# Query, key and value projections as five fp16 products of high and low parts instead of two fp32 ones

## The chip, the cores and the metric

The kernel runs on one core of one Trainium2 chip. The metric is the device time of one execution in microseconds (us); the time before is the median of three runs. The profile is one further execution.

## The reference, cut to what matters

Sixteen images of 192 channels on a 32 x 32 grid (1024 tokens) pass through three layers, each added to its input: a gated recurrent mix over rows and columns, a windowed attention, and a mixture of four experts of which two are chosen for each token. The change touches the first step of the attention:

```python
def _L1_attn_ref(x, Wq, bq, Wk, bk, Wv, bv, Wo, bo):   # x: LayerNorm over the 192 channels of each token
    H, D = (6, 32)
    WIN = 33
    def proj(W, b):
        return (x @ W + b).reshape(B, L, H, D).transpose(0, 2, 1, 3)
    Q, K, V = (proj(Wq, bq), proj(Wk, bk), proj(Wv, bv))
    ...
    # token 0 attends to all tokens; every other token to the 33 around it and to token 0
```

So per image three products of a 1024 x 192 matrix with a 192 x 192 matrix.

## The kernel before

**Images as a pipeline.** No scheduler orders the work: every engine has its own program, written out by hand, and semaphores join them. For image i the program runs `attention(i)`, then `experts(i)`, which works through four blocks of 512 routed tokens (24 chunks, each a first product `ffn1` into 768/6 = 128 hidden channels and a second, `ffn2`, out of them). Beside the chunks of image i, the generator `between(i)` prepares the next images: the rest of image i's attention, the group norm and the state projection (`project_states`, PROJ) of image i+2, and for image i+1 the token norm, its transposes, the windows, and the projections to queries, keys and values. `Slots` say at which step of `between` each part stands; the table `STEPS` says how many steps are taken after each half chunk. The last steps are taken at three per chunk. Images 0, 1 and 2 are prepared with no or few chunks beside them (`between(-1)`, `between(0)`, `between(1)`, where image 1 has one block only); the other 13 images are prepared beside 24 chunks.

**The projections before.** ScalarE writes the normed tokens to XN (128 tokens x 8 tiles x 192, fp32; line 787). TensorE waits for them (`xn1_ready`) and for the gates of image i+2 to have left its PSUM banks (`gu_ready`), and turns XN in two steps of eight transposes (`turn_mixed`, line 1493), halves j = 0, 1 of 96 channels. ScalarE copies half 0 and VectorE half 1 out of PSUM as overlapping windows (`windows`, lines 488 to 494): XW holds, for each of 11 blocks of 93 tokens, the 125 tokens around it and token 0, 126 columns. Then come 18 pieces (`project`, lines 1503 to 1519): 6 for Q and 6 for K, each 4 (or 3) blocks wide, 372 (279) or 504 (378) columns, with two products (j = 0, 1) of a 96-column weight each, and 6 for V, each two blocks of 126 tokens as the weight and the 192 columns of WV moving. Four PSUM banks take turns, so piece n waits for piece n-4 to be read. ScalarE reads the even pieces and VectorE the odd ones (`evacuate_piece`, lines 513 to 532), adding the bias.

**What stands around them.** In the last seven chunks the program of TensorE is: `ffn1` of chunk n, two pieces, `ffn2` of chunk n-1, one piece. `ffn2` waits for `split` on VectorE (HHI, HLO, lines 1054 and 1057), which waits for the gelu on ScalarE (line 810), which waits for `ffn1`. VectorE's order is split, then its pieces; ScalarE's is gelu, then its pieces. The chunks' own products are fp16 already, with high and low parts: five of 512 columns in `ffn1` (line 1532), twelve of 192 columns in `ffn2` (lines 1550 to 1552).

Of the kernel before, what the change touches and what calls it, by code (L numbers as in the profile page):

```python
# [67 lines left out]
def window_view(t, offset, dims):  # L68

    base = t[:]  # L70
    return bass.AP(tensor=base.tensor, offset=base.offset + offset, ap=[[base.ap[0][0], dims[0]]] + dims[1:])


def hybrid_kernel(nc, x, proj_w, y_wa, y_wb, y_scale, eye, gavg, cavg, norm_w, norm_b, g1_wT, g1_b, g2_wT, bias_row,
                  scan_v, scan_u, scan_a, wq, wk, wv, wo, bq, bk, bv, mask, w1, w2, b1, gate_w, gate_b, before, after,
                  consts, tri, out, powers, slots, weights):
    ctx = ExitStack()
    with ctx:
# [8 lines left out]
        EYEB = sb("EYEB", [128, QS], BF16)  # L87
# [8 lines left out]
        WQ, WK, WV, WO = (sb(n, [128, 2, C]) for n in ("WQ", "WK", "WV", "WO"))  # L96
# [106 lines left out]
        PSUM = ctx.enter_context(nc.psum_tensor("PSUM", [128, 8, 512], F32))  # L203


        with ExitStack() as setup:
# [276 lines left out]
        def windows(copy, j, part, give):  # L483

            if part == 0:
                copy(XW[0:HC, j, 1:NB - 1, 0:KW],
                     window_view(PSUM, j * T + QB - PAD + 1, [HC, [QB, NB - 2], [1, KW]]))
                return  # L490
            copy(XW[0:HC, j, 0, PAD - 1:KW], window_view(PSUM, j * T, [HC, [1, KW - PAD + 1]]))
            last = (NB - 1) * QB - PAD + 1
            copy(XW[0:HC, j, NB - 1, 0:T - last], window_view(PSUM, j * T + last, [HC, [1, T - last]]))
            copy(XW[0:HC, j, :, KW], window_view(PSUM, j * T, [HC, [0, NB]])).then_inc(give, 1)

# [1360 lines left out]
```

## Time and profile before

| | |
|---|---|
| median of 3 runs | 3102.83 us (3099.03 to 3105.12) |
| the profiled execution | 3101.95 us, its span 3100.2 us |
| TensorE (PE) busy | 2628.2 us, 85% of the span |
| VectorE (DVE) busy | 1836.3 us, 59% |
| ScalarE (ACT) busy | 1124.6 us, 36% |
| chain that ended last | PE 67%, DVE 19%, ACT 4%, issue 4% |

PE is a matmul, PEld a load of its stationary operand, which overlaps matmuls. Ends of matmuls are modelled and include their latency, so what a matmul costs in a row of them is the distance of the starts, not its duration. An fp32 matmul stands in the trace as two records. Lines are those of the kernel before.

### The profile page before, as it was taken

The page shows a single profiled execution, that of the slowest core. Times are in us where ns is not written, and L with a number is a line of the kernel's source. Part 1 is how long each engine was busy: PE and PEld are TensorE (multiplying, and loading weights), DVE is VectorE, ACT ScalarE, POOL GpSimd, SP SyncE. Part 2 cuts the span into 40 slices and gives each one's busy share as a digit, 9 for nine tenths or more (in the row PEclk, how much of TensorE's full clock was granted, in tenths as well). Part 3 has the DMA queues.
Part 4 walks back from the last instruction along what each step waited for, and adds up shares of the span by engine and source line. Part 5 has one row for each costly group of instructions (what it writes and reads, how often), then busy time and mean ns, then how long its engine had stood idle before and what let it go on. Part 6 is the DMA issues. An engine that isn't in the chain of part 4 may idle for free.

```text
span 3100.2 us, 49397 instructions
## 1 busy us (share of the span) xinstructions
PE 2628.2 (85%) x17619; PEld 1919.8 (62%) x17619; DVE 1836.3 (59%) x5182; ACT 1124.6 (36%) x3347; POOL 815.0 (26%) x656
## 2 busy tenths in 40 slices
PE   1359797999898999999898999999998989998397
PEld 0237575767676676667676666767576766766264
DVE  4345464656666565656666665756666666656354
ACT  0024243434343434434343434334343434343122
POOL 0000021223232322223232312232232322232344
PEclk9769788999999999998999999999989999999699
DMA  2430011324224242324333242423242241414464
GB/s 39 92 116 14 23 53 26 93 65 103 67 60 110 35 115 49 91 66 103 71 83 85 40 128 30 118 54 94 65 103 65 50 122 23 126 36 136 117 152 101
DMA packets 272628, 241.72 MB, mean 78 GB/s; under 512 B 209020, under 2 KB 250494, under 8 KB 261760
## 3 DMA queue, kind: packets, MB, share of 16 engines
q1 hardware_dynamic: 211648, 147.17, 17.8%
q0 software_dynamic: 50880, 52.59, 10.3%
q10 hardware_dynamic: 9856, 38.80, 3.9%
q8 instruction: 141, 2.31, 0.3%
q14 instruction: 103, 0.84, 0.1%
HBM read 133.29 MB, written 73.59 MB: 67 GB/s over the span
## 4 chain that ended last, share of the span: by engine, by line
PE 67%; DVE 19%; ACT 4%; issue 4%; DMA 1%; POOL 1%; SPq 1%; ACTq 0%; DVEq 0%; POOLq 0%
PE PSUM L1532 10%; PE PSUM L1509 9%; PE PSUM L1580 7%; PE PSUM L1602 5%; PE PSUM L1550 4%; PE PSUM L1518 3%; PE PSUM L1552 3%; PE PSUM L1551 3%; DVE HLO L1057 3%; PE PSUM L1448 3%; PE PSUM L1404 2%; PE PSUM L1592 2%; DVE HHI L1054 2%; PE PSUM L1445 2%; PE PSUM L1677 2%
## 5 line engine op out<-in xcount | busy, mean ns | idle before, releaser
L1532 PE MATMUL PSUM<-XT,WB 128*128 128x512 f16 x2010 | 522.8, 393 | 46.9 <-DMA META<-slots 43.5
L702 POOL DMA_INDIRECT out_dram<-Y,META x228 | 363.5, 1594 | 643.9 <-DVE Y L1081 517.6
L842 ACT ACTIVATE PSPT<-PSUM,NMX 94x126 f32<-94x126 f32 x1056 | 367.1, 358 | 370.8 <-PE PSUM L1592 188.0
L810 ACT ACTIVATE HF<-PSUM,WB 128x512 f32<-128x512 f32 x402 | 273.9, 685 | 526.6 <-PE PSUM L1532 525.7
L1550 PE MATMUL PSUM<-WB,HHI 128*128 128x192 f16 x1608 | 400.8, 249 | 48.7 <-DVE HLO L1057 47.5
L1551 PE MATMUL PSUM<-WB,HHI 128*128 128x192 f16 x1608 | 399.1, 248 | 0.0
L1552 PE MATMUL PSUM<-WB,HLO 128*128 128x192 f16 x1608 | 399.0, 248 | 0.0
L1054 DVE TENSOR_SCALAR HHI<-HF 128x512 f16<-128x512 f32 x402 | 172.3, 429 | 354.2 <-ACT HF L810 351.8
L1532 PEld LDWEIGHTS PSUM<-XT,WB 128*128 128x128 f16 x2010 | 197.3, 101 | 227.2 <-issue 47.1
L1580 PE MATMUL PSUM<-KBD,QT 128*94 128x378 f32 x704 | 308.4, 522 | 9.7 <-ACT PSPT L842 8.1
L1057 DVE SCALAR_TENSOR_TENSOR HLO<-HF,HHI 128x512 f16<-128x512 f32 x402 | 278.3, 692 | 13.8
L687 POOL DMA_INDIRECT slots<-XROW,IDX x256 | 251.7, 983 | 82.8 <-issue 76.3
L1602 PE MATMUL PSUM<-VW,PSPT 126*94 126x32 f32 x2112 | 220.5, 257 | 33.4 <-DVE PSPT L1092 32.3
L1602 PEld LDWEIGHTS PSUM<-VW,PSPT 126*94 126x94 f32 x2112 | 206.1, 175 | 53.4 <-DVE PSPT L1092 53.3
L1550 PEld LDWEIGHTS PSUM<-WB,HHI 128*128 128x128 f16 x1608 | 160.4, 100 | 125.4 <-issue 67.1
L1108 DVE TENSOR_REDUCE NMX<-PSUM 94x3 f32<-94x378 f32 x352 | 185.1, 543 | 72.9 <-PE PSUM L1583 70.5
L842 ACT ACTIVATION_READ_ACCUMULATOR PSPT<-PSUM,NMX 94x1 f32 x1056 | 209.3, 198 | 0.0
L1099 DVE TENSOR_TENSOR XW<-PSUM,RDEN 94x192 f32<-94x192 f32 x176 | 62.3, 354 | 197.6 <-PE PSUM L1602 195.1
L658 POOL TENSOR_TENSOR TR<-TV,MHALF 128x4 f32<-128x4 f32 x32 | 34.0, 1063 | 541.7 <-DVE TV L940 541.7
L1551 PEld LDWEIGHTS PSUM<-WB,HHI 128*128 128x128 f16 x1608 | 159.0, 99 | 20.6 <-issue 11.1
L1592 PEld LDWEIGHTS PSUM<-EYE,PSPT 94*126 94x126 f32 x1056 | 113.0, 150 | 83.0 <-issue 77.5
L1552 PEld LDWEIGHTS PSUM<-WB,HLO 128*128 128x128 f16 x1608 | 158.8, 99 | 0.3
(270 smaller groups left out, 4542.6 us busy)
## 6 DMA issues: line engine op xcount, KB each, us to landing
WB<-weights SPq DMA_DIRECT2D x67, 1600.0 KB, 6.9
XR<-in_x ACTq DMA_DIRECT2D x16, 768.0 KB, 5.2
out_dram<-X ACTq DMA_DIRECT2D x32, 384.0 KB, 3.0
weights<-WB ACTq DMA_DIRECT2D x4, 1600.0 KB, 6.1
GUP<-TGU SPq DMA_DIRECT2D x256, 8.0 KB, 1.8
slots<-XROW,IDX POOLq DMA_INDIRECT x256
out_dram<-Y,META POOLq DMA_INDIRECT x228, 3.6
HF<-in_w ACTq DMA_DIRECT2D x6, 384.0 KB, 4.6
```

The source lines that it names most:

```text
L687: pool.indirect_dma_start(slots[:, :].bitcast(I32), bass.IndirectOffsetOnAxis(IDX[:, k, t:t + 1], 0), XROW[:, t, :].bitcast(I32), None, bo ...
L702: pool.indirect_dma_start(out[:, :], bass.IndirectOffsetOnAxis(row, 0), Y[:, wslot(i, j), q, :], None, bounds_check=B * T + BS - 1, oob_is ...
L810: act.activation(HF[:, k % 2, :], PSUM[:, 4 + k % 2, :], ACT.Gelu, scale=1 / (X_UP * W_UP), bias=bias).then_inc(f["gelu_done"], 1)
L842: e = act.activation(PS[0:QS, n % 2, h, :], PSUM[0:QS, n % 2, h * KS:(h + 1) * KS], ACT.Exp, bias=NMX[:, b, n % 2, h:h + 1], accum_out=DEN ...
L1057: dve.scalar_tensor_tensor(HLO[:, k % 2, :], HF[:, k % 2, :], H_UP, HHI[:, k % 2, :], ALU.mult, ALU.subtract).then_inc(f["hl_ready"], 1)
L1509: mm = pe.matmul(PSUM[0:HC, n % 4, 0:width], W[:, j, oh * HC:(oh + 1) * HC], XW[:, j, b0:b1, keys], start=(j == 0), stop=(j == 1))
L1532: mm = pe.matmul(dst, WB[:, ws, w:w + 128], XT[:, xs, chunk, :], start=(n == 0), stop=(n == 4))
L1550: pe.matmul(dst, HHI[:, k % 2, tok], w2h, start=False, stop=False, skip_group_check=True)
L1551: pe.matmul(dst, HHI[:, k % 2, tok], w2l, start=False, stop=False, skip_group_check=True)
L1552: mm = pe.matmul(dst, HLO[:, k % 2, tok], w2h, start=False, stop=(k == HK - 1), skip_group_check=True)
L1580: pe.matmul(PSUM[0:QS, n % 2, 0:HH * KS], QT[:, oh, b, :], KBD[:, oh, b, :, :].rearrange("p h k -> p (h k)"), start=True, stop=False)
L1602: mm = pe.matmul(PSUM[0:QS, 2, O_COL + c:O_COL + c + HD], PT[:, n % 2, h, :], VW[:, b, c:c + HD], start=True, stop=True)
```

## The change

Every fp32 value times a scale (1024 for the tokens, 64 for the weights) is written as a high fp16 part and a low fp16 part, the rest. A product of 192 channels then is (high + low)(high + low) without low times low: 3 x 192 = 576 rows of contraction, and with pieces of 64 channels laid in pairs on 128 partitions it takes five products of 128 rows, where fp32 took two of 96. The weights are split once, in the setup, on VectorE (WQKV). The tokens are split per image: ScalarE writes the high part of four tiles after the four tiles of XN, VectorE the low part (`low_part`), between its two parts of the gates. The transposes are of 128 x 128 fp16 and three per tile instead of two; the windows are of three parts c = 0, 1, 2 on 128 partitions, of which ScalarE copies 0 and 2 and VectorE copies 1. VectorE also zeroes the edges of the windows. The pieces' readers divide by the scales.

```diff
-        WQ, WK, WV, WO = (sb(n, [128, 2, C]) for n in ("WQ", "WK", "WV", "WO"))
+        WO = sb("WO", [128, 2, C])
+        WQKV = sb("WQKV", [128, 3, 5, C], F16)
...
-        XW = sb("XW", [128, 2, NB, KS])
+        XWF = sb("XW", [128, NB * C])
+        XW = XWF[:].bitcast(F16)[:, 0:3 * NB * KS].rearrange("p (a b k) -> p a b k", a=3, b=NB)
...
-        VW = sb("VW", [KS, NB, C])
+        VWF = sb("VW", [128, NB * C])
+        VW = VWF[0:KS, :].rearrange("p (b c) -> p b c", b=NB)
+        XH = VWF[:].bitcast(F16)[:, 0:NT * 2 * C].rearrange("p (t c) -> p t c", t=NT)
...
+        PSUMH = PSUM[:].rearrange("p a b -> p (a b)").bitcast(F16)
...
-                    (WQ[0:HC], wq), (WK[0:HC], wk), (WV[0:HC], wv), (WO[:], wo), (BQ[:], bq), (BK[:], bk), (BV[:], bv),
+                    (WB[:].rearrange("p a b -> p (a b)").bitcast(F32)[:, 0:9 * C], wqkv), (WO[:], wo), (BQ[:], bq), (BK[:], bk), (BV[:], bv),
...
+                    dve.tensor_copy(EYEH[:], EYE[:])
+                    wide = WB[:].rearrange("p a b -> p (a b)").bitcast(F32)[:, 0:9 * C].rearrange(
+                        "p (m k c) -> p m k c", m=3, k=3)
+                    for k, high in ((0, 0), (1, 2), (2, 3)):
+                        link(dve.tensor_scalar(WQKV[:, :, high, :], wide[:, :, k, :], W_UP, None, ALU.mult))
+                    for k, high, low in ((0, 0, 1), (1, 2, 4)):
+                        dve.scalar_tensor_tensor(WQKV[:, :, low, :], wide[:, :, k, :], W_UP, WQKV[:, :, high, :],
+                                                 ALU.mult, ALU.subtract)
...
+                return copy(XW[:, c, 1:NB - 1, 0:KW],
+                            window_view(PSUMH, c * T + QB - PAD + 1, [128, [QB, NB - 2], [1, KW]]))
+            copy(XW[:, c, 0, PAD - 1:KW], window_view(PSUMH, c * T, [128, [1, KW - PAD + 1]]))
+            copy(XW[:, c, NB - 1, 0:T - LAST_KEY], window_view(PSUMH, c * T + LAST_KEY, [128, [1, T - LAST_KEY]]))
+            return copy(XW[:, c, :, KW], window_view(PSUMH, c * T, [128, [0, NB]]))
...
+        CHUNKS = (0, 0, 1, 2, 1)
+        UNSCALE = 1 / (X_UP * W_UP)
...
                     a.then_inc(s["xn1_ready"], 1)
+                    act.wait_ge(s["xn1_ready"], at("xn1_ready", i, k + 1))
+                    tiles = slice(4 * k, 4 * k + 4)
+                    act.activation(XH[:, tiles, 0:C], XN[:, tiles, 0:C], ACT.Copy, scale=X_UP).then_inc(s["xn1_high"], 1)
                     yield from slot.until(XN1_SLOT + 1 + k)
...
                 act.wait_ge(s["xn1T_done"], at("xn1T_done", i, 1))
-                windows(act.copy, 0, 0, s["win_act"])
+                windows(act.copy, 0, 0)
+                windows(act.copy, 0, 1)
                 yield from slot.until(WINDOW_SLOT + 1)
-                windows(act.copy, 0, 1, s["win_act"])
+                windows(act.copy, 2, 0)
+                windows(act.copy, 2, 1).then_inc(s["win_act"], 1)
...
+            def low_part(i, k):
+
+                tiles = slice(4 * k, 4 * k + 4)
+                dve.wait_ge(s["xn1_high"], at("xn1_high", i, k + 1))
+                dve.scalar_tensor_tensor(XH[:, tiles, C:2 * C], XN[:, tiles, 0:C], X_UP, XH[:, tiles, 0:C], ALU.mult,
+                                         ALU.subtract).then_inc(s["xn1_low"], 1)
...
+                dve.memset(XW[:, :, 0, 0:PAD - 1], 0.0)
+                dve.memset(XW[:, :, NB - 1, T - LAST_KEY:KW], 0.0)
+                windows(dve.tensor_copy, 1, 0)
                 yield from slot.until(WINDOW_SLOT + 1)
-                windows(dve.tensor_copy, 1, 1, s["win_dve"])
+                windows(dve.tensor_copy, 1, 1).then_inc(s["win_dve"], 1)
...
-                    for kind in range(2):
-                        yield from slot.until(STATE_SLOT + 1 + kind)
-                        gated_states(i + 2, kind)
+                for k in range(2):
+                    yield from slot.until(STATE_SLOT + 1 + k)
+                    if has(i + 2):
+                        gated_states(i + 2, k)
+                    if has(i + 1):
+                        low_part(i + 1, k)
...
-                pe.wait_ge(s["xn1_ready"], at("xn1_ready", i, k + 1))
+                pe.wait_ge(s["xn1_low"], at("xn1_low", i, k + 1))
                 for t in range(4 * k, 4 * k + 4):
-                    for j in range(2):
-                        mm = pe.transpose(PSUM[0:HC, 2 * j + t // 4, (t % 4) * 128:(t % 4 + 1) * 128],
-                                          XN[:, t, j * HC:(j + 1) * HC], EYE[:])
+                    for c in range(3):
+                        mm = pe.transpose(PSUMH[:, c * T + t * 128:c * T + (t + 1) * 128],
+                                          XH[:, t, c * 128:(c + 1) * 128], EYEH[:])
...
-                    for j in range(2):
-                        mm = pe.matmul(PSUM[0:HC, n % 4, 0:width], W[:, j, oh * HC:(oh + 1) * HC],
-                                       XW[:, j, b0:b1, keys], start=(j == 0), stop=(j == 1))
+                    for k, c in enumerate(CHUNKS):
+                        mm = pe.matmul(PSUM[0:HC, n % 4, 0:width], WQKV[:, n // 6, k, oh * HC:(oh + 1) * HC],
+                                       XW[:, c, b0:b1, keys], start=(k == 0), stop=(k == 4))
...
-                        for j in range(2):
-                            mm = pe.matmul(PSUM[0:KS, n % 4, (b % 2) * C:(b % 2 + 1) * C], XW[:, j, b, :],
-                                           WV[:, j, :], start=(j == 0), stop=(j == 1))
+                        for k, c in enumerate(CHUNKS):
+                            mm = pe.matmul(PSUM[0:KS, n % 4, (b % 2) * C:(b % 2 + 1) * C], XW[:, c, b, :],
+                                           WQKV[:, 2, k, :], start=(k == 0), stop=(k == 4))
```

**VectorE, the gates and the windows.** On VectorE, beside the last chunks of an image (an image in the middle of the program), this stands before the change (TGU is the gates of image i+2, L1054 and L1057 the split of a chunk, XW the windows, QT the first piece):

```order
L989 SCALAR_TENSOR_TENSOR TGU<-TGU,PSUM 16x32x32 [waits i_tanh_done]
L994 SCALAR_TENSOR_TENSOR TGU<-TGU,PSUM 16x1024 [waits i_tanh_done]
L1054 TENSOR_SCALAR HHI<-HF 128x512 [waits b_ffn2_chunk,b_gelu_done]
L1057 SCALAR_TENSOR_TENSOR HLO<-HF,HHI 128x512 [waits b_hh_ready]
L488 COPY XW<-PSUM 96x9x125 [waits i_xn1T_done]
L1054 TENSOR_SCALAR HHI<-HF 128x512 [waits b_ffn2_chunk,b_gelu_done]
L1057 SCALAR_TENSOR_TENSOR HLO<-HF,HHI 128x512 [waits b_hh_ready]
L491 COPY XW<-PSUM 96x110
L493 COPY XW<-PSUM 96x109
L494 COPY XW<-PSUM 96x11
```

and this after it, at the same place (line numbers are the changed kernel's; VW is the memory that XH, the split tokens, shares):

```order
L1007 SCALAR_TENSOR_TENSOR TGU<-TGU,PSUM 16x32x32 [waits i_tanh_done]
L1058 SCALAR_TENSOR_TENSOR VW<-XN,VW 128x4x192 [waits i_xn1_high]
L1012 SCALAR_TENSOR_TENSOR TGU<-TGU,PSUM 16x1024 [waits i_tanh_done]
L1058 SCALAR_TENSOR_TENSOR VW<-XN,VW 128x4x192 [waits i_xn1_high]
L1081 TENSOR_SCALAR HHI<-HF 128x512 [waits b_ffn2_chunk,b_gelu_done]
L1084 SCALAR_TENSOR_TENSOR HLO<-HF,HHI 128x512 [waits b_hh_ready]
L1064 MEMSET XW 128x3x15 [waits i_xn1T_done]
L1065 MEMSET XW 128x3x16
L497 COPY XW<-PSUM 128x9x125
L1081 TENSOR_SCALAR HHI<-HF 128x512 [waits b_ffn2_chunk,b_gelu_done]
L1084 SCALAR_TENSOR_TENSOR HLO<-HF,HHI 128x512 [waits b_hh_ready]
```

The first low part now stands ahead of the second gate, the second low part ahead of the chunk's split, and two small memsets ahead of the window.

**ScalarE, the windows.** On ScalarE, same place (L810 and L828 are the gelu of a chunk), before:

```order
L488 COPY XW<-PSUM 96x9x125 [waits i_xn1T_done]
L810 ACTIVATE HF<-PSUM,WB 128x512 [waits b_hl_ready,b_ffn1_done]
L491 COPY XW<-PSUM 96x110
L493 COPY XW<-PSUM 96x109
L494 COPY XW<-PSUM 96x11
```

and after:

```order
L497 COPY XW<-PSUM 128x9x125 [waits i_xn1T_done]
L499 COPY XW<-PSUM 128x110
L500 COPY XW<-PSUM 128x109
L501 COPY XW<-PSUM 128x11
L828 ACTIVATE HF<-PSUM,WB 128x512 [waits b_hl_ready,b_ffn1_done]
L497 COPY XW<-PSUM 128x9x125
L499 COPY XW<-PSUM 128x110
L500 COPY XW<-PSUM 128x109
L501 COPY XW<-PSUM 128x11
```

The small copies of part 0 moved ahead of the gelu, and a whole further part follows it.

## Rows read from the trace of the kernel before

**Rows 1.** Part 1 of the page: busy time, share, instructions.

```profile
PE 2628.2 (85%) x17619; PEld 1919.8 (62%) x17619; DVE 1836.3 (59%) x5182; ACT 1124.6 (36%) x3347; POOL 815.0 (26%) x656
```

**Rows 2.** Busy time by stretch: PE, PEld, DVE, ACT, POOL, granted clock, DMA share, GB/s.

```profile
647.70:664.10 16.40, 12.45 (x71) 8.46 (x70) 8.65 (x12) 8.92 (x16) 7.26 (x5) 0.90 0.39 45
...
996.00:1012.00 16.00, 10.81 (x71) 7.09 (x70) 9.79 (x15) 8.86 (x15) 7.20 (x5) 1.00 0.40 44
1012.00:1048.00 36.00, 35.82 (x190) 23.19 (x191) 15.85 (x29) 11.91 (x21) 6.45 (x4) 1.00 0.12 14
```

**Rows 3.** The chain from 640 to 720: start, time on the chain, what.

```profile
641.24 1.68 PE PSUM L1677 x16
...
657.43 1.94 PE PSUM L1493 x8
...
661.07 0.87 PE PSUM L1493 x8
...
668.07 2.20 PE PSUM L1509 x8
670.27 0.26 PE PSUM L1513 x4
...
671.54 1.26 PE PSUM L1509 x4
672.80 1.08 PE PSUM L1532 x5
...
678.07 1.69 PE PSUM L1509 x4
...
680.84 2.96 PE PSUM L1509 x8
...
693.92 2.60 PE PSUM L1518 x16
```

**Rows 4.** Groups by line and shape: count, busy us, mean ns, idle before.

```profile
L1550 PEld LDWEIGHTS PSUM<-WB,HHI 128*128 128x128 f16 x1608 | 160.4, 100 | 125.4 <-issue 67.1 <-DVE HHI L1054 51.7
...
L526 DVE TENSOR_SCALAR KBD<-PSUM,BK 32x504 f32<-32x504 f32 x96 | 70.6, 735 | 71.7 <-PE PSUM L1509 69.2
...
L1583 PEld LDWEIGHTS PSUM<-MASKB,EYEB 128*94 128x94 bf16 x352 | 45.2, 128 | 60.1 <-issue 60.1
...
L1177 DVE SCALAR_TENSOR_TENSOR XROW<-XN,XROW 128x768 f16<-128x768 f32 x32 | 30.7, 959 | 1.1
```

**Rows 5.** Timeline of TensorE: start, length, line, shape, count, idle before.

```profile
1001.23 0.25 PE L1550 MATMUL PSUM<-WB,HHI 128*128 128x192 f16 x1
...
1002.22 1.24 PE L1532 MATMUL PSUM<-XT,WB 128*128 128x512 f16 x5
1005.66 1.08 PE L1493 MATMUL PSUM<-EYE,XN 128*96 128x128 f32 x8 [2.20 <-DVE TGU L994]
1007.57 1.04 PE L1493 MATMUL PSUM<-EYE,XN 128*96 128x128 f32 x8
...
1012.18 1.47 PE L1509 MATMUL PSUM<-XW,WQ 128*96 128x372 f32 x4 [1.51 <-DVE XW L494]
```

**Rows 6.** Timelines of VectorE and of ScalarE in the same stretch.

```profile
1004.39 1.21 DVE L994 SCALAR_TENSOR_TENSOR TGU<-TGU,PSUM 16x1024 f32<-16x1024 f32 x1
...
1008.64 1.33 DVE L488 COPY XW<-PSUM 96x1125 f32<-96x1125 f32 x1 [1.85 <-PE PSUM L1493]
...
1011.87 0.16 DVE L494 COPY XW<-PSUM 96x11 f32<-96x11 f32 x1
...
1008.64 1.09 ACT L488 COPY XW<-PSUM 96x1125 f32<-96x1125 f32 x1 [2.19 <-PE PSUM L1493]
1009.72 0.69 ACT L810 ACTIVATE HF<-PSUM,WB 128x512 f32<-128x512 f32 x1
...
1010.58 0.19 ACT L494 COPY XW<-PSUM 96x11 f32<-96x11 f32 x1
```

**Rows 7.** Timeline of VectorE in the setup of the expert weights.

```profile
143.13 0.76 DVE L1358 SCALAR_TENSOR_TENSOR WB<-HF,WB 128x576 f16<-128x576 f32 x1
```

More of the change, by code:

```diff
@@ L68, in window_view @@
 def window_view(t, offset, dims):
-    base = t[:]
+    base = t
     return bass.AP(tensor=base.tensor, offset=base.offset + offset, ap=[[base.ap[0][0], dims[0]]] + dims[1:])
 def hybrid_kernel(nc, x, proj_w, y_wa, y_wb, y_scale, eye, gavg, cavg, norm_w, norm_b, g1_wT, g1_b, g2_wT, bias_row,
-                  scan_v, scan_u, scan_a, wq, wk, wv, wo, bq, bk, bv, mask, w1, w2, b1, gate_w, gate_b, before, after,
+                  scan_v, scan_u, scan_a, wqkv, wo, bq, bk, bv, mask, w1, w2, b1, gate_w, gate_b, before, after,
                   consts, tri, out, powers, slots, weights):
@@ L86, in hybrid_kernel @@
         EYE = sb("EYE", [128, 128])
-        EYEB = sb("EYEB", [128, QS], BF16)
+        EYEB, EYEH = sb("EYEB", [128, QS], BF16), sb("EYEH", [128, 128], F16)
         GAVG = sb("GAVG", [HC, HC])
@@ L274, in link @@
                         dve.wait_ge(dve_step, n_dve[0])
-                    for t in (XW, KBD, XG, PSPT):
+                    for t in (XWF, KBD, XG, PSPT):
                         dve.memset(t[:], 0.0)
-                    for t in (WQ, WK, WV, QT):
-                        dve.memset(t[96:128], 0.0)
+                    dve.memset(QT[96:128], 0.0)
                     dve.memset(WY[:], 0.0)
@@ L481, in hybrid_kernel, with windows @@
         STEPS = [(1, 0) if n < 14 else (1, 1) if n < 16 else (2, 1) for n in range(NSEL * HK)] + [(1, 1)]
-        def windows(copy, j, part, give):
+        def windows(copy, c, part):
             if part == 0:
[L488 to L494, printed above, removed]
+                return copy(XW[:, c, 1:NB - 1, 0:KW],
[3 more added lines that the diff above has]
+            return copy(XW[:, c, :, KW], window_view(PSUMH, c * T, [128, [0, NB]]))
+        LAST_KEY = (NB - 1) * QB - PAD + 1
+        CHUNKS = (0, 0, 1, 2, 1)
+        UNSCALE = 1 / (X_UP * W_UP)
         SPANS = [(0, 4), (4, 8), (8, NB)]
@@ L512, in evacuate_piece @@
                     if is_act:
-                        last = eng.activation(dst, ps, ACT.Identity, bias=BQS[:, oh:oh + 1], scale=HD ** -0.5)
+                        last = eng.activation(dst, ps, ACT.Identity, bias=BQS[:, oh:oh + 1], scale=UNSCALE * HD ** -0.5)
                     else:
-                        last = eng.tensor_scalar(dst, ps, BQ[:, oh:oh + 1], HD ** -0.5, ALU.add, ALU.mult)
+                        last = eng.tensor_scalar(dst, ps, UNSCALE * HD ** -0.5, BQS[:, oh:oh + 1], ALU.mult, ALU.add)
             elif n < 12:
@@ L523, in evacuate_piece @@
                     if is_act:
-                        last = eng.activation(dst, ps, ACT.Identity, bias=BK[p, oh:oh + 1])
+                        last = eng.activation(dst, ps, ACT.Identity, bias=BK[p, oh:oh + 1], scale=UNSCALE)
                     else:
-                        last = eng.tensor_scalar(dst, ps, BK[p, oh:oh + 1], None, ALU.add)
+                        last = eng.tensor_scalar(dst, ps, UNSCALE, BK[p, oh:oh + 1], ALU.mult, ALU.add)
             else:
@@ L531, in evacuate_piece @@
                 ps = src[0:KS, 0:k * C].rearrange("p (b q) -> p b q", b=k)
-                last = eng.copy(dst, ps) if is_act else eng.tensor_copy(dst, ps)
+                if is_act:
+                    last = eng.activation(dst, ps, ACT.Copy, scale=UNSCALE)
+                else:
+                    last = eng.tensor_scalar(dst, ps, UNSCALE, None, ALU.mult)
             last.then_inc(give, 1)
@@ L1777, in halves, with paired @@
         return np.ascontiguousarray(w.reshape(2, HC, -1).transpose(1, 0, 2))
+    def paired(w):
+        parts = w.reshape(3, C // 3, C)
+        return np.concatenate([np.concatenate([parts[p], parts[q]]) for p, q in ((0, 1), (2, 0), (1, 2))], 1)
     def vec(v):
@@ L1833 @@
         scan_v=sv, scan_u=su, scan_a=sa,
-        wq=halves(a["L1_attn_Wq"]), wk=halves(a["L1_attn_Wk"]), wv=halves(a["L1_attn_Wv"]), wo=np.concatenate([halves(a["L1_attn_Wo"]), wo_rows]),
+        wqkv=np.concatenate([paired(a["L1_attn_W" + n]) for n in "qkv"], 1), wo=np.concatenate([halves(a["L1_attn_Wo"]), wo_rows]),
         bq=vec(a["L1_attn_bq"]), bk=vec(a["L1_attn_bk"]), bv=vec(a["L1_attn_bv"]),
```

12 lines of the change are left out of this document (5 added, 7 removed).

## The prediction

> **What bounds the kernel now.** I read the page first: TensorE is busy for 85% of the span, VectorE for 59%, ScalarE for 36% [rows 1]. An average over stages says little, so I looked at the stage of the change by stretches. From 1012 to 1048 us, where one image's pieces stand beside the last chunks of the image before it, TensorE is busy 35.82 of 36 us at full clock, while VectorE works 15.85 and ScalarE 11.91 us [rows 2]: that stage is bound by TensorE alone, so time taken from it there is time won, until another engine becomes the bound. The 16 us ahead of it are different: TensorE is busy 10.81 us of them [rows 2], and the timeline names two waits of the turning work: 2.20 us for the second gate on VectorE (L994) before the transposes, and 1.51 us for the last window copy before the first piece [rows 5]. There the bound is a chain through VectorE and ScalarE, and the change adds work to exactly that chain. So I cost both stages, for 13 images beside chunks and for three with few or none.
>
> **Products removed.** The chain gives the time that records really take. Q is (1.26 + 2.20 + 0.26) x 2 = 7.44 us per image, K is (1.69 + 2.96) x 2 = 9.30 us, and V, 44 records of which 16 take 2.60 us, is 7.15 us [rows 3]. Together 23.9 us.
>
> **Products added.** An fp16 product of 512 columns takes 1.08 / 5 = 0.216 us [rows 3]. Twelve of 192 columns stand between 1001.23 and 1002.22 us, 0.0825 us each [rows 5]. The line through both is 0.417 ns a column plus 2.5 ns. So Q: 20 products of 372 columns at 0.1575 and 10 of 279 at 0.119 make 4.34 us, and ten of a single column, which are bound by the load of their weights, some 0.75 us (four such cost 0.26 us now, rows 3, and only part of a load shows in them): 5.1 us. K: 20 of 504 at 0.2125 and 10 of 378 at 0.160: 5.85 us. Loads of 96 columns hide under all of these.
>
> **V is where the count misleads.** Its 55 products of 192 columns could take 0.0825 us each, as ffn2's do, if their loads hide. But their weight is 126 token columns wide, not 128. In the trace the 16-bit load of 94 columns lasts 128 ns, and the one of 128 columns, though wider, only 100 [rows 4]. Two kinds of 16-bit load, then, and 128 columns have the quick one. What a slow load costs when nothing covers it shows where 16 records with 128-column fp32 weights move only 4 columns each: 1.68 / 16 = 0.105 us, the first being partly covered [rows 3]. The bounds for a product of V are 0.0825 us, if 126 columns load as quickly as 128, and 0.11 us; I take 0.108, since the 94-column row is the only 16-bit load here that is not 128 wide. V: 55 x 0.108 = 5.9 us. Under fp32 the same slow load was hidden, because a record streamed for 0.1625 us (2.60 / 16, rows 3).
>
> The Trainium skill has the rule in its page "TensorE: Matmul & The Clock Gate": section "Weight-path perf modes — Fast Weight Load (FWL) and DoubleRow" has the fast load only for exactly 128 weight columns of a type other than fp32, and section "LDWEIGHTS (loading the stationary operand)" gives columns / 1.2 ns for the ordinary one. For 126 columns that is an estimate of 105 ns, so 5.8 us for V; by a count of streamed columns alone it would be 4.5 us. The trace agrees with the rule as far as 94 against 128 columns go.
>
> Sum of the added products: 5.1 + 5.85 + 5.9 = 16.9 us, against 23.9: **7.0 us less on TensorE per image**.
>
> **The gates and the low parts.** The first low part stands ahead of the second gate. The same operation on the same shape (768 columns, fp32 in, fp16 out) takes 0.959 us [rows 4]. The second gate now ends at 1004.39 + 1.21 = 1005.60 us [rows 6] and TensorE starts 0.06 later, so its wait grows from 2.20 to about 3.16 us. Behind that gate stand the second low part and the chunk's split; the second half of the transposes needs the low part, but an ffn2 of 12 x 0.0825 = 1.0 us covers it. ScalarE's two high parts (bounds: 1.09 x 768/1125 = 0.75 us by the window copy of rows 6, and that copy's 1.09 us) push a gelu back by 1.6 to 2.2 us, some two microseconds before anything asks for it: nothing. Transposes: eight cost (1.08 - 0.27) / 7, about 0.11 us each, now, 1.75 us in all; 24 with quick loads and 128 columns come by the line to 24 x 0.056 = 1.35 us, with slow loads to 2.6. I take 1.35: their weight is 128 wide.
>
> **The windows.** With turns ending about 0.5 us later than now (0.96 late, 0.4 faster), copying starts near 1009.1 instead of 1008.64 us. ScalarE takes 1.09 for part 0; its three small copies now end at 1010.77, 0.36 after the gelu [rows 6], so I give them 0.45. Then comes the gelu, at about 1010.7 instead of 1009.72, 0.69, and 1.09 + 0.45 for part 2: with start-ups about 1012.9. VectorE's last copy stands behind a split that waits for that gelu, ends now at 1012.03 [rows 6], and moves with the gelu to about 1013.0. The first piece starts at about 1013.1 instead of 1012.18 [rows 5]: **0.9 us lost**. A faster copy of 16-bit data on VectorE would not help, because ScalarE ends as late.
>
> **Clock.** The first two stretches of rows 2 are the same steps of two images, and one ran at 0.90 mean granted clock, the other at 1.00. In the first the time from one turn's start to the other's is 661.07 - 657.43 = 3.64 us [rows 3], in the other 1007.57 - 1005.66 = 1.91 [rows 5]: one fall to 1.2 GHz costs 1.7 us. With a longer wait I expect it in nearly every image rather than about half of them, and a few more after the wait before the first piece: 0.7 of an image more, 1.2 us.
>
> **The end of the stage.** ScalarE's last gelu stands behind the V piece 16, and the last ffn2 needs it. So the 0.3 us that pieces 16 and 17 save (12 records x 0.1625 against 15 products x 0.108) is given back.
>
> **Do the readers keep up?** A K piece is read on VectorE by three instructions of 0.735 us [rows 4], 2.2 us. In six K pieces VectorE owes 3 of these (the last is narrower), some 6.3 us, and two splits, 2.3 us, while TensorE now needs 5.85 us for the pieces and 2 x 2.07 us for the halves of two chunks: 8.6 against 10.0 us. It fits by 14%, with four banks of slack. Cost zero; if that cover is gone, it is a rival below.
>
> **Sum.** Beside chunks: 7.0 - 0.9 - 0.3 - 1.2 = 4.6 us x 13 = 60. The three images without: the same 7.0, less 0.96 for the gate and 1.3 for ScalarE's extra part (2 x 1.54 = 3.1 against VectorE's 1.33 and small copies like ScalarE's), 4.7 x 3 = 14. Setup: five instructions over 576 columns at 0.76 us or less each [rows 7], and 0.43 MB more to load (at the 44 GB/s that the thinner stretch of rows 2 moved 10 us, at nothing if it lands beside the other loads; I take 1.5): 5 us, all on the setup's chain. Together 60 + 14 - 5 = 69 us. The profiled execution took 3101.95 us (span 3100.2), 0.9 below the median; 3102.8 - 69 = **3034 us**.
>
> **Rivals.**
> *Quick V loads.* 126 columns load as 128 do: V is 4.5 us, 1.4 more saved x 16 = 22 us, 3012 us. Against it stands the 94-column row. 0.17.
> *Everything hidden.* Quick loads and no loss at windows or clock: 8.4 x 16 - 5 = 129, 2974 us. The two named waits speak against it. 0.04.
> *The readers become the bound.* VectorE's split for a chunk stands behind a 2.2 us K evacuation, and TensorE stands at ffn2 for it. If each of the three K chunks loses 0.8 us, 2.4 x 16 = 38 us: 3072 us. For it: only 14% margin. Against: TensorE asks for a split a whole period after its ffn1. 0.16.
> *Slower, by the clock.* The wait of 3.2 us and the 2.1 us one soon after could hold the clock at 1.2 GHz into the pieces. Every microsecond of full-speed work done there at half clock costs one more. The gain per image beside chunks is used up after 69 / 13 = 5.3 us of such work; if half of the 29 us stage ran low, 13 x 14 = 180 us, 3215 us. Against: after the 2.20 us waits it was back within one turn [rows 3]: the second turn took 0.87 us. 0.04.
> *No net change*, by several prices of the setup and windows at their upper ends: 0.02.
> The forecast: 0.57.
>
> **How the numbers follow.** The forecast's own range is 3015 to 3055 (clock 0 to 2.4 us an image, windows 0 to 1.8, transposes at either bound). With quick loads below and bound readers above, 3004 to 3072 holds 0.8. A measurement of this kernel tells 0.2%, 6 us. Faster 0.94, same 0.02, slower 0.04.
>
> **What would show it.** V products 0.105 to 0.11 us apart; Q and K at 0.16 and 0.21; the wait before the transposes 3.1 to 3.2 us, before the first piece about 2; more stretches at 0.9 clock ahead of the pieces; no wait of TensorE between the first and the last piece; piece stage 7 us shorter. I would be wrong if TensorE waits for HLO or a reader in the K pieces, or if the low clock reaches into them.

## The result, and the profile after

The changed kernel takes 2992.42 us (median of 4, 2983.7 to 2994.43), the one before 3102.5 us in the same comparison (3099.03 to 3105.12): a ratio of 0.964, 95% interval 0.9619 to 0.9662. That is 110 us less, where 69 were forecast; 2992 lies under the range of 3004 to 3072. The profiled execution has a span of 2990.4 us.

Part 1 of the page of the changed kernel, which answers to [rows 1]:

```profile
PE 2495.5 (83%) x18147; PEld 1873.5 (63%) x18147; DVE 1863.1 (62%) x5249; ACT 1173.0 (39%) x3443; POOL 811.2 (27%) x656
```

TensorE has 133 us less of busy time, and VectorE and ScalarE carry the splits, 27 and 48 us more. Next, busy time by stretch, as in [rows 2] (length; PE, PEld, DVE, ACT, POOL; granted clock, DMA share, GB/s; a granted clock of 1.00 is 2.4 GHz, 0.50 is 1.2 GHz). The first row goes from one image's first transposes to its first piece. The second is the next image, from the state projection that runs ahead of its transposes (it belongs to the image after it; below it is called an image's projection) to its first piece, and the third that image's piece stage:

```profile
803.47:812.22 8.75, 7.33 (x54) 5.96 (x54) 4.34 (x11) 3.60 (x9) 0.00 (x0) 0.67 0.13 20
...
961.96:977.22 15.26, 10.34 (x79) 6.71 (x79) 9.55 (x16) 10.22 (x19) 6.20 (x4) 1.00 0.35 38
977.22:1007.75 30.53, 29.50 (x241) 22.29 (x242) 17.34 (x31) 14.32 (x24) 6.22 (x4) 1.00 0.21 36
```

The piece stage, from the first piece to the first scores, is 30.53 us. Before, the same stage is this row of the same view:

```profile
1012.18:1051.30 39.12, 38.32 (x216) 25.39 (x217) 17.20 (x31) 14.40 (x24) 6.45 (x4) 1.00 0.17 28
```

So the stage is 8.59 us shorter, and TensorE is still busy for all but 1.03 of its 30.53 us. The timeline of TensorE (start, length, line, shape, count, idle before) for two images after, to be read against [rows 5]:

```profile
803.47 1.46 PE L1523 MATMUL PSUM<-EYEH,VW 128*128 128x128 f16 x12 [3.20 <-DVE TGU L1012]
806.64 1.49 PE L1523 MATMUL PSUM<-EYEH,VW 128*128 128x128 f16 x12
...
812.22 0.97 PE L1538 MATMUL PSUM<-XW,WQKV 128*96 128x372 f16 x5 [1.42 <-DVE XW L501]
...
970.93 0.84 PE L1523 MATMUL PSUM<-EYEH,VW 128*128 128x128 f16 x12 [3.20 <-DVE TGU L1012]
...
972.60 0.83 PE L1523 MATMUL PSUM<-EYEH,VW 128*128 128x128 f16 x12
...
977.22 0.97 PE L1538 MATMUL PSUM<-XW,WQKV 128*96 128x372 f16 x5 [1.72 <-DVE XW L501]
...
1003.34 1.40 PE L1547 MATMUL PSUM<-WQKV,XW 128*126 128x192 f16 x15
1004.58 0.25 PE L1579 MATMUL PSUM<-WB,HHI 128*128 128x192 f16 x1
...
1006.76 0.24 PE L1579 MATMUL PSUM<-WB,HHI 128*128 128x192 f16 x1 [1.03 <-DVE HLO L1084]
```

Both waits that the prediction named are there. Of the 13 images prepared beside chunks, the first 12 wait alike, 3.19 to 3.20 us each; the last has no gates behind it and waits 4.1 us for a low part. These 12 are the images counted below. In the image at 803 us the clock is down around the transposes, for 6.8 us from 1.1 us ahead of them (0.67 mean in the stretch above): one turn to the next takes 3.17 instead of 1.67 us, and the way to the first piece 8.75 instead of 6.29. A spell, below, is such a stretch at half clock. The row to stop at is the one at 1003.34: 15 V products start in 1.24 us, **0.083 us each**, not 0.108.

VectorE and ScalarE in the same stretch, which answer to [rows 6]:

```profile
968.67 0.96 DVE L1058 SCALAR_TENSOR_TENSOR VW<-XN,VW 128x768 f16<-128x768 f32 x1
969.65 1.21 DVE L1012 SCALAR_TENSOR_TENSOR TGU<-TGU,PSUM 16x1024 f32<-16x1024 f32 x1
...
973.68 0.75 DVE L497 COPY XW<-PSUM 128x1125 f16<-128x1125 f16 x1
...
976.88 0.19 DVE L501 COPY XW<-PSUM 128x11 f16<-128x11 f16 x1
...
974.80 0.72 ACT L828 ACTIVATE HF<-PSUM,WB 128x512 f32<-128x512 f32 x1
975.39 1.13 ACT L497 COPY XW<-PSUM 128x1125 f16<-128x1125 f16 x1
```

The low part takes 0.96 us ahead of the second gate, as costed from [rows 4]. VectorE's window copy takes 0.75 us, 1.33 before.

### The profile page after: what moved, and what is told of

Same layout as the page of the kernel before. It is cut to its first block, busy times and chain, and to the rows that moved or that the text cites. A ratio compares the mean times of both kernels' runs of the same rounds, so it can differ in the third digit from the quotient of the medians.

```text
span 2990.4 us, 50614 instructions
## 1 busy us (share of the span) xinstructions
PE 2495.5 (83%) x18147; PEld 1873.5 (63%) x18147; DVE 1863.1 (62%) x5249; ACT 1173.0 (39%) x3443; POOL 811.2 (27%) x656
## 4 chain that ended last, share of the span: by engine, by line
PE 65%; DVE 20%; ACT 5%; issue 4%; DMA 1%; POOL 1%; SPq 1%; ACTq 0%; DVEq 0%; POOLq 0%
PE PSUM L1561 10%; PE PSUM L1609 7%; PE PSUM L1538 5%; PE PSUM L1631 5%; PE PSUM L1579 4%; PE PSUM L1581 3%; PE PSUM L1580 3%; DVE HLO L1084 3%; PE PSUM L1478 3%; PE PSUM L1434 2%; PE PSUM L1547 2%; DVE HHI L1081 2%; PE PSUM L1621 2%; PE PSUM L1475 2%; PE PSUM L1706 2%
## 5 line engine op out<-in xcount | busy, mean ns | idle before, releaser
L1561 PE MATMUL PSUM<-XT,WB 128*128 128x512 f16 x2010 | 529.2, 396 | 48.9 <-DMA META<-slots 43.5
L828 ACT ACTIVATE HF<-PSUM,WB 128x512 f32<-128x512 f32 x402 | 274.0, 686 | 530.1 <-PE PSUM L1561 529.0
L1538 PE MATMUL PSUM<-XW,WQKV 128*96 128x372 f16 (+3 forms) x960 | 189.9, 343 | 29.5 <-DVE XW L501 20.6
L1538 PEld LDWEIGHTS PSUM<-XW,WQKV 128*96 128x96 f16 x960 | 117.6, 126 | 85.0 <-ACT XW L501 32.9
```

The source lines that it names most:

```text
L828: act.activation(HF[:, k % 2, :], PSUM[:, 4 + k % 2, :], ACT.Gelu, scale=1 / (X_UP * W_UP), bias=bias).then_inc(f["gelu_done"], 1)
L1538: mm = pe.matmul(PSUM[0:HC, n % 4, 0:width], WQKV[:, n // 6, k, oh * HC:(oh + 1) * HC], XW[:, c, b0:b1, keys], start=(k == 0), stop=(k == 4))
L1561: mm = pe.matmul(dst, WB[:, ws, w:w + 128], XT[:, xs, chunk, :], start=(n == 0), stop=(n == 4))
```

## Experiments

Each is an edit of the changed kernel. To compare with it: 2992 us, ratio 0.964 (0.9619 to 0.9662) to the kernel before. Every ratio below is to the kernel before too, which took 3099.5 to 3100.5 us beside them.

**What a load costs.**

```
+ for _ in range(60):                       # full-clock products of 378 columns, once, ahead of all groups
+     pe.matmul(PSUM[:, 6, 0:378], ONESB[:], MASKB[:, 1, :], ...)
+ for width, columns in ((128, 4), (126, 4), (96, 4), (64, 4), (128, 192), (126, 192)):
+     for _ in range(16):
+         pe.matmul(PSUM[0:width, 7, 0:columns], ONESB[:, 0:width], MASKB[:, 1, 0:columns], ...)
+ ...  # EYEH (fp16) and EYE (fp32) of 128, 126, 96 columns with 4 moving columns
```

> The changed kernel with groups of 16 products added to its setup, each after 60 full-clock products of 378 columns: bf16 weights of 128, 126, 96 and 64 columns with 4 moving columns, bf16 weights of 128 and 126 columns with 192 moving columns, fp16 weights of 128, 126 and 96 columns with 4 moving columns, and fp32 weights of 128, 126 and 96 columns with 4 moving columns. It tells what a load costs where nothing covers it. Theory A (only fp32 loads are slow; a 16-bit load goes in at about one column per 2.4 GHz cycle at every width): 128, 126, 96 and 64 columns of 16-bit weights start 55, 54, 42 and 30 ns apart, with 192 moving columns both widths 83 ns apart, fp32 of 128 and 126 columns 105 ns or more. Theory B (my prediction's: a width other than 128 takes the slow load, but the V products of the changed kernel hide it in some way): 126 columns with 4 moving columns start 105 to 110 ns apart, 96 columns 80 ns apart, against about 30 to 55 ns for 128. What decides is the distance of starts within a group at full clock.

The 60 products stand once, ahead of the first group, and not ahead of each, and the clock fell twice among the groups. The kernel ran once, 3037.59 us with these products in its setup, and that time is compared with nothing. Groups of its setup by line and shape (count, busy us, mean ns of one, idle), and then the granted clock by stretch, the third figure from the right:

```profile
L386 PE MATMUL PSUM<-EYE 128*128 128x4 f32 x32 | 3.7, 253 | 0.0
...
L379 PE MATMUL PSUM<-MASKB,ONESB 128*126 128x4 bf16 x16 | 1.1, 197 | 0.0
L383 PE MATMUL PSUM<-EYEH 128*126 128x4 f16 x16 | 1.1, 197 | 0.0
...
L383 PE MATMUL PSUM<-EYEH 128*96 128x4 f16 x16 | 0.9, 184 | 0.0
...
L383 PE MATMUL PSUM<-EYEH 128*128 128x4 f16 x16 | 0.5, 164 | 0.0
```

```profile
56.00:59.20 3.20, 3.20 (x61) 2.81 (x60) 0.00 (x0) 0.00 (x0) 0.00 (x0) 1.00 0.02 5
59.20:62.60 3.40, 3.40 (x33) 3.25 (x32) 0.00 (x0) 0.00 (x0) 0.00 (x0) 0.50 0.00 0
62.60:65.80 3.20, 3.20 (x63) 3.20 (x63) 0.00 (x0) 0.00 (x0) 0.00 (x0) 1.00 0.00 0
65.80:69.40 3.60, 3.60 (x37) 3.60 (x35) 0.00 (x0) 0.00 (x0) 0.00 (x0) 1.00 0.02 5
```

The busy time of a group is its starts plus one length, so 126 columns of 16-bit weights start (1.1 - 0.197) / 15 = 60 ns apart (57.5 by the starts themselves), 96 columns 48 (45), 128 columns 22 (25). The fp32 group holds two records for each of its 16 products, (3.7 - 0.253) / 31 = 111 ns each. All of these ran at full clock. With 192 moving columns, 126 columns start 82 ns apart at full clock; the 128-column group with 192 fell into the half-clock row and tells nothing. Theory A holds where it decides: 126 and 96 columns cost 57.5 and 45 ns (54 and 42 expected), far from theory B's 105 and 80, and 57.5 ns fits under 192 moving columns. On the 128-column load theory A was wrong, 25 ns and not 55, and what theory B kept of the prediction, that a width other than 128 takes a slower load, is so.

**V's weights 128 columns wide.**

```
+ dve.memset(...)                           # the two columns behind the last window
...
- mm = pe.matmul(PSUM[0:KS, n % 4, ...], XW[:, c, b, :], ...)
+ mm = pe.matmul(PSUM[:, n % 4, ...], XWF[:].bitcast(F16)[:, first_key:first_key + 128], ...)
```

> The changed kernel with V's weights read 128 columns wide instead of 126 (the two extra columns are the start of the next window, their two rows of the result are read by nobody; one more memset of 2 columns per image). Theory A (the width of 126 costs nothing beside 192 moving columns): V products stay 83 ns apart and the time stays within 3 us of 2992. Theory B (126 columns pay something for the slow load that the start distances hide, at most the 1 or 2 ns a product by which they could differ from ffn2's): 55 x 2 ns x 16 = 1.8 us less at most. If the load of 126 columns cost what I predicted, 25 ns a product, this kernel would be 22 us faster, about 2970. I expect 2990 to 2995.

2996.9 us (2983.68 to 3004.22), ratio 0.9655 (0.963 to 0.968): no difference from the changed kernel that can be told, and none of the 22 us that the predicted price would have given back. The windows and the loads by shape in its piece stage:

```profile
977.82:1008.35 30.53, 29.49 (x241) 22.21 (x242) 17.35 (x31) 14.32 (x24) 6.23 (x4) 1.00 0.21 34
```

```profile
L1549 PEld LDWEIGHTS PSUM<-WQKV,XW 128*128 128x128 f16 x55 | 4.6, 98 | 0.5
```

The same loads last 136 ns each at 126 columns in the changed kernel. Their record became 38 ns shorter and the stage stayed at 30.53 us. The length of a load's record is not its price.

**Three products instead of five.**

```
- for k, c in enumerate(CHUNKS):
+ for k, c in ((0, 0), (2, 1), (3, 2)):
```

> The changed kernel with three products a piece in place of five (the two of high part by high part order zero and one that start the sum and the first of the low parts are left: products 1, 3 and 4 of the five; the second and the fifth are left out, so the result is less exact). Theory A (TensorE alone bounds the piece stage): Q, K and V lose two fifths of their time, (4.34 + 0.45 + 5.85 + 4.54) x 0.4 = 6.1 us per image, 97 us in all: 2895 us, and no wait of TensorE in the piece stage. Theory B (the readers are near their limit, 14% of margin by my sum in the K pieces): there VectorE's 8.6 us stand against TensorE's 3.5 + 4.1 = 7.6, so TensorE waits some 1 us in the K pieces of each image, and perhaps as much in Q and V: 16 to 40 us of the 97 are lost, 2911 to 2935 us, with waits for L536 or L525 (VectorE) or HLO between pieces.

2940.85 us (2930.32 to 2947.01), ratio 0.9496 (0.9481 to 0.951): 51 us less, where B's smallest gain was 57. One image's piece stage, and the waits of TensorE in it, 955.9 to 981.7 us (total, times, longest):

```profile
955.94:981.64 25.70, 23.77 (x191) 17.35 (x192) 17.18 (x31) 14.11 (x24) 6.20 (x4) 1.00 0.26 41
```

```profile
PE PSUM L1579 <- DVE HLO L1084: 1.2, 1, 1.2
PE PSUM L1547 <- DVE KBD L536: 0.6, 1, 0.6
```

The stage is 25.70 us, 4.84 less instead of 6.1, and a wait for a K reader appears, 0.6 us ahead of a V piece, where five products have none. With the longer wait for HLO that is 0.8 of the 1.3 us that are missing; the other 0.5 is not accounted for. So the readers stand about where the prediction put them: no bound at five products, a small one at three. From one image's projection to the next it is only 4.07 us less. The trace says where the rest went: the stretch from an image's first scores to the next projection, which the edit doesn't touch, takes 119.1 us on average, 118.05 in the changed kernel, with 15.5 us at half clock against 14.3.

**Both low parts ahead of the gates.**

```
+ if has(i + 1):
+     yield from slot.until(STATE_SLOT)
+     for k in range(2):
+         low_part(i + 1, k)
  for k in range(2):
      yield from slot.until(STATE_SLOT + 1 + k)
      if has(i + 2):
          gated_states(i + 2, k)
-     if has(i + 1):
-         low_part(i + 1, k)
```

> The changed kernel with both low parts ahead of the two gates, one slot earlier on VectorE, where it waits some 2.9 us for a gelu now. Theory A (the low part between the gates makes TensorE's wait before the transposes 1 us longer, and the longer wait takes the clock down for longer): the wait goes back from 3.20 to about 2.2 us, 1.0 us x 14 images = 14 us, and the low clock between that wait and the first piece falls from 1.43 to about 0.8 us of lost time per image, another 8 us: about 2970. Theory B (the wait is paid back later, as the window copies or a gelu end no earlier): the wait before the first piece grows by what the other shrinks, and the time stays at 2990 or more. A third case: the second low part delays the split ahead of it by 0.35 us and that ffn2 waits; then 2975 to 2980.

2970.93 us (2964.22 to 2972.42), ratio 0.958 (0.9567 to 0.9593). Theory A has this to a microsecond, by its mechanism but with luck in the size, as shown below. Its TensorE timeline:

```profile
969.38 0.84 PE L1525 MATMUL PSUM<-EYEH,VW 128*128 128x128 f16 x12 [2.21 <-DVE TGU L1012]
...
975.67 0.97 PE L1540 MATMUL PSUM<-XW,WQKV 128*96 128x372 f16 x5 [1.72 <-DVE XW L501]
```

The wait is back at 2.21 us. Of the 12 images in the steady part, 2 have low clock ahead of the first piece (7.82 and 7.84 us there, the others 6.29), where the changed kernel has 8. So the clock costs 0.26 us per image, where the expectation had 0.8. With the 1.0 us of the wait the 12 images should have given 2.2 us each; from projection to projection they gave 1.93, the stretch behind the scores took 0.3 us more, and the first of them already began 2.9 us later than in the changed kernel's profile.

**Both waits filled with unread products.**

```
  if has(i + 2):
+     keep_busy(18, 3)
      pe.wait_ge(s["gu_ready"], at("gu_ready", i + 2, 2))
...
+ keep_busy(8, 3)
  pe.wait_ge(s["win_act"], at("win_act", i + 1, 1))
```

> The changed kernel with work that nobody reads put into TensorE's two waits: 18 products of 378 columns (0.158 us each, 2.85 us) ahead of the wait for the gates, which lasts 3.20 us, and 8 (1.3 us) ahead of the wait for the windows, 1.72 us. Nothing else moves. Theory A (the low clock between transposes and first piece comes from the idle time of those waits): the spells at half clock there go, 1.43 us per image on average over 13 images, and some of the low clock of images 1 and 2: 18 to 22 us less, 2970 to 2975. Theory B (the clock falls for another reason, or the added products run into the work behind them): 2990 or more, with spells of 3.4 and 6.8 us still ahead of the pieces.

2973.48 us (2969.97 to 2978.45), ratio 0.9593 (0.958 to 0.9606). All 12 images take 6.29 us from the transposes to the first piece: theory A. Which of the two waits it is, the next two kernels tell, each with one of the fills.

> The changed kernel with the 18 unread products in the wait for the gates only. If the wait of 3.20 us before the transposes is what takes the clock down: no low spell between transposes and first piece beside chunks (6.29 us in all 12 images), 2973 to 2977 as with both waits filled. If it is the wait of 1.72 us before the first piece: 6.29 to 8.75 us as now, and 2988 to 2995.

> The changed kernel with the 8 unread products in the wait for the windows only. If the first wait takes the clock down, the spell begins ahead of these products and goes on through them: the products run at half clock (8 x 0.315 = 2.5 us in a wait of 1.4 to 1.7) and delay the first piece by up to 1 us in images with a spell, so 2992 to 3000. If the second wait does it: 2975.

The gates' wait alone: 2977.28 us (2967.45 to 2977.9), ratio 0.9606 (0.959 to 0.9622), and again 6.29 us in all 12 images. The windows' wait alone: 3002.24 us (2996.04 to 3010.68), ratio 0.968 (0.9663 to 0.9696). Their rows, first with the first wait filled, then with the second:

```profile
805.86 0.84 PE L1523 MATMUL PSUM<-EYEH,VW 128*128 128x128 f16 x12 [0.35 <-DVE TGU L1012]
...
812.15 0.97 PE L1538 MATMUL PSUM<-XW,WQKV 128*96 128x372 f16 x5 [1.72 <-DVE XW L501]
```

```profile
976.28 1.46 PE L1523 MATMUL PSUM<-EYEH,VW 128*128 128x128 f16 x12 [3.20 <-DVE TGU L1012]
...
983.45 1.44 PE L1597 MATMUL PSUM<-MASKB,ONESB 128*128 128x378 bf16 x8
985.04 0.97 PE L1538 MATMUL PSUM<-XW,WQKV 128*96 128x372 f16 x5
```

It is the first wait. With only the second filled, the clock is down before the fill starts: spells in 9 of 12 images. My reason for a loss there was wrong, though: the eight products ran at full clock again, and the piece starts no later than in the changed kernel (8.76 us against 8.75 with the same spell). What is slower by 10 us lies elsewhere. In the profiles, whose runs differ by 18 us, image 1's projection starts at 344.4 us, against 335.5 in the changed kernel, image 3's at 636.3 against 630.8, and from there each stretch from scores to the next projection takes 119.1 us, 118.05 in the changed kernel, again with 15.5 us at half clock against 14.3.

**All windows but part 0 on VectorE.**

```
  windows(act.copy, 0, 0)
- windows(act.copy, 0, 1)
- yield from slot.until(WINDOW_SLOT + 1)
- windows(act.copy, 2, 0)
- windows(act.copy, 2, 1).then_inc(s["win_act"], 1)
+ windows(act.copy, 0, 1).then_inc(s["win_act"], 1)
...
- dve.wait_ge(s["xn1T_done"], at("xn1T_done", i, 1))
  dve.memset(...)                           # both
+ dve.wait_ge(s["xn1T_done"], at("xn1T_done", i, 1))
  windows(dve.tensor_copy, 1, 0)
- yield from slot.until(WINDOW_SLOT + 1)
- windows(dve.tensor_copy, 1, 1).then_inc(s["win_dve"], 1)
+ windows(dve.tensor_copy, 2, 0)
+ windows(dve.tensor_copy, 1, 1)
+ windows(dve.tensor_copy, 2, 1).then_inc(s["win_dve"], 1)
```

> The changed kernel with the third part of the windows copied by VectorE instead of ScalarE: VectorE copies parts 1 and 2 ahead of its split (two copies of 0.75 us and six small ones), its two memsets stand ahead of its wait for the transposes, and ScalarE copies part 0 alone. Theory A (what the first piece waits for is the copy of part 2 behind the gelu on ScalarE and VectorE's small copies behind the split that waits for the same gelu): the copies end 2.3 us after the transposes in place of 3.7, the wait of 1.72 us before the first piece falls to 0.4, 1.3 us per image beside chunks and somewhat more in the three others, 18 to 20 us: about 2973. Theory B (the copies on VectorE delay the split, and the last chunk's ffn2 asks for it): the gain is given back as a wait for HLO, and the time stays within 5 us of 2992.

2985.16 us (2980.23 to 2995.0), ratio 0.963 (0.9612 to 0.9648): 7 us, not 18 to 20, and since the interval overlaps the changed kernel's (0.9619 to 0.9662), not even the 7 are clear of noise. The wait ahead of the first piece went as theory A has it, and the clock took part of the gain:

```profile
973.25 0.84 PE L1521 MATMUL PSUM<-EYEH,VW 128*128 128x128 f16 x12 [3.20 <-DVE TGU L1009]
...
975.57 1.48 PE L1521 MATMUL PSUM<-EYEH,VW 128*128 128x128 f16 x12
...
979.31 0.97 PE L1536 MATMUL PSUM<-XW,WQKV 128*96 128x372 f16 x5
```

No wait stands ahead of the first piece any more, and it comes 6.06 us after the first transposes. But the wait of 3.20 us is still there, and now all 12 images have a spell of low clock behind it, 3.4 or 6.8 us long, against 8 of 12. On average the stretch is 6.46 us, 7.72 in the changed kernel: 1.26 x 13 = 16 us less, of which the median shows 7. In the profile image 3's projection starts 4.3 us later than in the changed kernel's, and from image 14's projection to image 15's first scores it takes 3.8 us longer; why, no run tells. Both together, low parts first and windows on VectorE, then with the fills:

> Both low parts ahead of the gates, and the windows copied as in the run before. If the two waits are separate and each is paid in full: 21 us of the first (2971 measured against 2992) and 18 to 20 of the second, so about 2953. If the first wait's end only moves the second's work to a gelu that isn't ready, the sum falls short: 2960 to 2970.

2959.72 us (2954.34 to 2959.85), ratio 0.9538 (0.9525 to 0.9551): 33 us under the changed kernel, more than the 21 and 7 of the two alone (the 7 with the noise said above) and less than the 39 expected. The stretch is now 4.76 us in all 12 images.

> As the run before, with 11 unread products of 378 columns (1.74 us) in the wait for the gates, which is then about 2.2 us, and 2 in the wait for the windows. If what is left of the low clock comes from these waits: 3 to 5 us less than that run, about 2949. If that run has no low clock there any more, the same time within 3 us, or up to 3 us more where the fill is longer than a wait.

2945.64 us (2941.61 to 2951.22), ratio 0.9499 (0.9485 to 0.9513): 47 us under the changed kernel and 155 under the one before, with nothing left out of the computation. It is 14 us less than the run before, where 3 to 5 were expected at most. Beside chunks it takes the same 43.3 us from projection to scores as the run before. What the fills add lies in images 1 and 2, from projection to scores 31.3 and 31.1 us against 34.3 and 33.4, and in the stretch from an image's scores to the next projection, 0.8 us an image (118.4 us, 14.0 at half clock, against 119.1 and 15.8). From the timelines, without and with the fills:

```profile
963.51 0.84 PE L1523 MATMUL PSUM<-EYEH,VW 128*128 128x128 f16 x12 [2.20 <-DVE TGU L1009]
...
968.27 0.97 PE L1538 MATMUL PSUM<-XW,WQKV 128*96 128x372 f16 x5 [0.19 <-DVE XW L501]
```

```profile
953.68 1.92 PE L1597 MATMUL PSUM<-MASKB,ONESB 128*128 128x378 bf16 x11
956.08 0.84 PE L1523 MATMUL PSUM<-EYEH,VW 128*128 128x128 f16 x12 [0.48 <-DVE TGU L1009]
```

## Where the prediction was right and where wrong

**The step that failed** is "V is where the count misleads": "I take 0.108, since the 94-column row is the only 16-bit load here that is not 128 wide." Measured: 0.083. It rested on two misreadings. The first: the 128 ns of the 94-column row in [rows 4] is the length of a load's record, which is no price: V's own loads last 136 ns while they start 83 ns apart, and going to 98 ns with 128 columns moved nothing. The second: the 0.105 us of [rows 3] was a price of fp32 weights, taken for that of a 16-bit load. Uncovered, an fp32 record takes 111 ns, a 16-bit load of 126 columns 57.5, and that fits under the 83 ns of 192 moving columns. V cost 4.5 us per image instead of 5.9, and that alone is 1.4 x 16 = 22 us of the 41 missed. The rival "quick V loads", held at 0.17, is what happened, for another reason than it gave: the load of 126 columns is slower than that of 128, and hidden all the same. Its 3012 us is still 20 us more than measured; that lies in the terms below.

The Trainium skill, page "TensorE: Matmul & The Clock Gate", section "LDWEIGHTS (loading the stationary operand)", prices a load at columns / 1.2 ns, an estimate of 105 ns for 126 columns. The measured 57.5 ns for a 16-bit load at full clock does not fit; the measurement decides. Its section "Weight-path perf modes — Fast Weight Load (FWL) and DoubleRow" gives a fast load to 128 columns of a type other than fp32. The load experiment agrees: 25 ns between starts at 128 columns of bf16 or fp16, 57.5 at 126.

**Terms that were mis-sized.** The ten products of one column cost 0.45 us, not 0.75 (45 ns each, the uncovered load of 96 columns). With V, the products added come to 15.2 us, not 16.9, and TensorE saves 8.7 us, not 7.0. The clock costs 0.64 us more per image than before (1.43 against 0.80 on average over 12 images), not 1.2, and in another way than forecast: there are spells in 8 images of 12, not in nearly all (6 of 12 before), and five of the 8 last 6.8 us and cost some 2.45 us each, where a spell before the change cost 1.6. With one profile of each kernel the counts are rough: 9, 8 and 9 of 12 in the profiles of the kernels with wide V weights, three products and the second fill, which have the same wait. The setup's five instructions take 3.2 us in all, and most of it is covered. The first rows are the setup of the changed kernel, the last its first group mean:

```profile
38.09 1.74 DVE L303 TENSOR_SCALAR WQKV<-WB 128x576 f16<-128x576 f32 x3
39.86 1.43 DVE L305 SCALAR_TENSOR_TENSOR WQKV<-WB,WQKV 128x576 f16<-128x576 f32 x2
```

```profile
96.00 0.48 PE L1423 MATMUL PSUM<-MV,GAVG 96*96 96x2 f32 x2 [31.94 <-DVE MV L977]
```

Before, that group mean starts at 95.63 us behind a wait of 33.84: 0.4 us lost, not 5, the rest being covered by a load that lands no earlier. The 0.4 holds for these two profiles: in the nine experiments with this same setup the group mean starts at 96.4 to 99.7 us.

**Terms that held.** The gates: 3.20 us of wait, 3.16 forecast, and back at 2.21 once the low parts were moved. The windows: from projection to first piece at full clock 15.26 us, 14.49 before, so 0.8 lost, 0.9 forecast. The tail: the last ffn2's wait for HLO grew from 0.8 to 1.03 us, about the 0.3 given back. The transposes at 0.056 us each: 12 in 0.68 (970.93 to the ffn2 at 971.61). The readers: no wait for them in the piece stage with five products, and one of 0.6 us with three.

**The sum with what was measured**, per image beside chunks: 8.7 - 0.25 - 0.8 - 0.64 = 7.0 us, and from one image's projection to the next it is 7.11 less (165.40 against 172.52). The 8.7 of TensorE and the 0.25 of the tail are the 8.59 of the piece stage, within 0.15 us. Over 13 images that is 92 us, 60 forecast. The setup and the three images without chunks gained 18 us together by the first scores of image 2 (515.84 against 533.89), 9 forecast. 92 + 18 = 110. The 41 us missed split by these terms into V 22, the one-column products 5 (0.3 x 16), the clock 7 (0.56 x 13), the setup 5 and the windows and the tail 2.

**What stays open.** The low clock of the other stages. Image 1's projection starts anywhere from 334.5 to 344.4 us in the profiles of kernels that do the same work up to there or nearly so. From an image's scores to the next projection the kernels take 117.3 to 119.1 us on average, with 11.2 to 15.8 us of it at half clock. A product of 378 columns starts every 0.315 us at half clock and every 0.160 at full clock in the load experiment, so half of the time at half clock is what the clock costs there, as an estimate. Take that off, and 110.9 to 111.7 us are left in every kernel, so most of what differs there is the clock. Why it is down longer in one kernel than in another is not shown, and so neither the 9 us that the windows' change seems to have lost again nor the 10 us of the second fill has a cause.

## What to carry to other kernels

Read the price of a load or a product from the distance between starts in a run of equal ones of the same type, never from the length of its record, and first see how many records a product has: fp32 has two here. When a helper step is put in front of something that TensorE waits for, look for idle time of its engine a slot earlier; here that was worth 21 us on top of the 110. And a wait of 3 us costs more than itself where the clock falls behind it: with unread products in that wait alone, the kernel was 15 us faster.

## What the runs showed of the hardware that was not expected

- At full clock, with 4 moving columns and nothing to cover them, 16-bit loads start 25 ns apart at 128 columns, 57.5 at 126 and 45 at 96. So 126 and 96 columns are dearer than 128 until something hides them; with 192 moving columns, 83 ns at 126 and at 128, the width makes no difference.
- An fp32 product of 128 columns and 4 moving ones is two records of 111 ns each.
- The clock fell from 2.4 to 1.2 GHz while TensorE had no gap by the profile (at 59.2 us in the load experiment, between the first two rows of its clock): what ran ahead of the fall were groups of 16 products with 4 moving columns each, back to back.
- Whether a wait is followed by a fall of the clock differs from image to image. Around the wait of 3.2 us there was a spell in 8 of 12, and in 12 of 12 in the kernel with all windows but part 0 on VectorE; around the wait of 2.2 us in 6 of 12 in the kernel before, in 2 and in 0 of 12 in the two kernels with the low parts first. These spells lasted 3.4 or 6.8 us; the longer ones began about 1 us before the wait ended.
- VectorE's copy of 128 x 1125 fp16 from PSUM took 0.75 us; 96 x 1125 fp32 took 1.33.
